# Rounding of the later batches as a chain over three engines, in a decoder layer on one Trainium2 core

## The reference

```
x = x + attention(layernorm(x))        # 32 heads, 8 key/value heads, causal, rotary
x = x + xattn(layernorm(x), context)   # the product below
x = x + moe(layernorm(x))              # 8 experts, capacity 256, plus a shared one, width 704

# xattn: both operands are rounded to float8 e4m3 in blocks, and scaled back
amax = max(abs(xb)) over 128 features of a token, at least 1e-4
q    = float8(xb * (448 / amax));  back = q * (amax / 448)
```

## Time and the profile before

| what | value |
|---|---|
| median of 3 runs | 1560.96 us (1559.98 to 1564.38) |
| profiled execution, its own time | 1559.33 us |
| its span, first to last instruction | 1557.5 us |
| mean granted TensorE clock | 0.982 |
| PE busy | 1445.0 us (93%) |
| DVE busy | 1188.3 us (76%) |
| POOL busy | 1024.0 us (66%) |
| ACT busy | 976.1 us (63%) |

### The profile page before, as it was taken

The page is one execution under the profiler, slowest core; times in us unless marked ns, Lnnn a source line. Parts: engine busy times, 40 slices in busy tenths (PEclk is TensorE's granted clock), DMA queues, the critical chain, the costliest instruction groups (busy, mean ns, idle before and its releaser), DMA issues.

```text
span 1557.5 us, 27023 instructions
## 1 busy us (share of the span) xinstructions
PE 1445.0 (93%) x8617; PEld 1263.8 (81%) x8617; DVE 1188.3 (76%) x2890; ACT 976.1 (63%) x2478; POOL 1024.0 (66%) x1027
## 2 busy tenths in 40 slices
PE   5899999999999999999999998977989897999997
PEld 4778888888878888778888887757888786999996
DVE  7678888887887887788888888787676755577775
ACT  4687777777677788878878787642121224556562
POOL 3787897887877888878988888434121213345455
PEclk9999999999999999999999999998999998999998
DMA  6435534333322433424434334222000004577777
GB/s 208 140 102 169 156 110 129 120 82 111 107 65 60 121 95 90 128 63 109 114 85 127 84 104 129 78 84 62 28 28 28 8 28 152 167 231 223 229 213 238
DMA packets 107964, 179.17 MB, mean 115 GB/s; under 512 B 17014, under 2 KB 38774, under 8 KB 107824
## 3 DMA queue, kind: packets, MB, share of 16 engines
q1 hardware_dynamic: 105072, 168.94, 37.0%
q0 software_dynamic: 2560, 8.25, 1.6%
q10 hardware_dynamic: 192, 0.26, 0.1%
HBM read 98.36 MB, written 33.03 MB: 84 GB/s over the span
## 4 chain that ended last, share of the span: by engine, by line
PE 62%; DVE 14%; ACT 12%; issue 6%; DMA 3%; POOL 2%; SPq 1%; DVEq 0%; POOLq 0%; ACTq 0%
PE bank L470 14%; PE bank L472 13%; PE bank L471 13%; PE bank L522 5%; ACT P L865 5%; PE bank L537 4%; PE bank L488 3%; PE bank L538 3%; PE bank L489 3%; DVE P L1191 2%; ACT PTh L877 2%; PE bank L462 2%; ACT Otmp L871 2%; DVE PTl L1232 1%; DVE Opair L1226 1%
## 5 line engine op out<-in xcount | busy, mean ns | idle before, releaser
L865 ACT ACTIVATE P<-P,mn 128x512 f32<-128x512 f32 (+3 forms) x512 | 284.5, 557 | 205.6 <-DVE mn L1191 201.8
L1636 POOL TENSOR_TENSOR P<-P,ri 128x128 f32<-128x128 f32 (+3 forms) x512 | 360.4, 735 | 30.8 <-DVE ri L1180 30.7
L1191 DVE CUSTOM_DVE_ANT_0 P<-bank,mask 128x512 f32<-128x512 f32 (+3 forms) x512 | 237.0, 481 | 84.1 <-PE bank L489 82.5
L1232 DVE TENSOR_TENSOR PTl<-bank,PTh 128x512 fp32r<-128x512 f32 (+1 forms) x384 | 229.9, 600 | 34.0 <-ACT PTh L877 31.3
L522 PE MATMUL bank<-ident,P 128*128 128x128 f32 x1280 | 201.4, 272 | 2.5 <-POOL P L1636 2.5
L877 ACT ACTIVATE PTh<-bank 128x512 fp32r<-128x512 f32 (+1 forms) x384 | 197.9, 517 | 3.5 <-PE bank L522 0.5
L488 PE MATMUL bank<-KT,QT 128*128 128x256 f32 (+2 forms) x512 | 187.6, 367 | 7.1 <-DVE mn L1191 7.1
L470 PE MATMUL bank<-XT,Wh 128*128 128x512 f32 x384 | 162.8, 424 | 9.2 <-DVE XT L1162 3.5
L537 PE MATMUL bank<-PTh,VS 128*128 128x256 f32 (+2 forms) x512 | 161.1, 326 | 6.8 <-DVE X L1241 2.4
L489 PE MATMUL bank<-KT,QT 128*128 128x256 f32 (+2 forms) x512 | 165.5, 323 | 0.0
L538 PE MATMUL bank<-PTl,VS 128*128 128x256 f32 (+2 forms) x512 | 154.6, 323 | 0.0
(11 more groups left out here) (224 smaller groups left out, 4160.5 us busy)
## 6 DMA issues: line engine op xcount, KB each, us to landing
RW<-in_wf SPq DMA_DIRECT2D x170, 256.0 KB, 3.0
QT<-qh SPq DMA_DIRECT2D x256, 64.0 KB, 2.0
QT<-ql SPq DMA_DIRECT2D x252, 64.0 KB, 2.0
Oraw<-in_wo SPq DMA_DIRECT2D x16, 512.0 KB, 4.7
KT<-KT SPq DMA_DIRECT2D x32, 256.0 KB, 3.0
Wraw<-in_wqkv SPq DMA_DIRECT2D x9, 768.0 KB, 5.0
xnx<-in_ctx SPq DMA_DIRECT2D x24, 256.0 KB, 3.6
saved<-Wh SPq DMA_DIRECT2D x7, 768.0 KB, 3.5
```

The costliest lines, as they stand in the source:

```text
L865: e.activation(pq, pq, ACT.Exp, bias=mn[:, z, qb:qb + 1], scale=-1.0, accum_out=rs[:, z, qb:qb + 1]).then_inc(a_exp, 1)
L1191: e.tensor_tensor_reduce(P[:, z, off[qb]:off[qb] + k], bank[n % 2][:, 0:k], mask[:, 512 - k:512], -0.125, BIG, ALU.add, ALU.min, mn[:, z, ...
L1232: e.tensor_tensor(pt_part(PTl, part), bank[2 + part][:, 0:128 * n].rearrange("p (m n) -> p m n", n=128), pt_part(PTh, part).bitcast(F32), ...
L1636: e.tensor_tensor(pq, pq, ri[:, z, qb:qb + 1].to_broadcast([128, n]), ALU.mult).then_inc(g_norm, 1)
```

## The change

For batches 1 to 3 the rounding is taken apart. ACT writes the normed tile (`look_later`, with a bias -mean/root that DVE computes once for a batch, `bias_of`); DVE takes its block maxima (`peaks`) one slot later; one set of scale steps serves all 4 tiles of a batch (`later_scales`); ACT multiplies by the scale, four activations to a tile (`scaled_later`); DVE's `rounded` keeps the two bit steps; POOL's three passes stay. The fourth tile of a batch is normed twice, for its maxima into the spare tile `T2[1]`, and again when its own buffer is free. A batch's first rounding is one slot earlier, its first transposes too; the fourth tile's come where they were. The scores and the choice of batch 0 move from slots -4 and -2 to -2 and 0, its places from 2 to 3.

```diff
-    plan(-4, "logits", 0)
-    plan(-2, "choose", 0)
-    plan(2, "place", 0)
+    plan(-2, "logits", 0)
+    plan(0, "choose", 0)
+    plan(3, "place", 0)
...
-            plan(s - 1 + i, "cross_round", b, i)
-            plan(s + 1 + i, "cross_turn", b, i)
-            plan(s + 2 + i, "cross_product", b, i)
-            plan(s + 3 + i, "stats3", b, i)
+
+            late = i // 3
+            plan(s - 8 + i, "look", b, i)
+            plan(s - 7 + i, "peaks", b, i)
+            plan(s - 3 + i + late, "scaled", b, i)
+            plan(s - 2 + i + late, "cross_round", b, i)
+            plan(s + i + late, "cross_turn", b, i)
+            plan(s + 1 + i + late, "cross_product", b, i)
+            plan(s + 2 + i + late, "stats3", b, i)
...
-        plan(s - 7, "norm2", b)
+        plan(s - 9, "norm2", b)
+        plan(s - 4, "scales", b)
...
+            def normed_by(dst, t):
+                e.activation(dst, X[:, t, :], ACT.Identity, bias=ssum[:, 0, t:t + 1],
+                             scale=rstd[:, t:t + 1]).then_inc(a_norm, 1)
+
+            def look_later(b, i):
+
+                need.wait_ge(v_small, 3 + 2 * b)
+                if i == 3:
+                    need.wait_ge(p_kv, NU)
+                    need.wait_ge(g_t2, TB * (b - 1))
+                    normed_by(T2[1], b * TB + i)
+                    return
+                need.wait_ge(p_turn, turn_at["cross_turn", b - 1, i or 3] + 1)
+                normed_by(T1[i], b * TB + i)
+
+            def scaled_later(b, i):
+                y = T1[i % 3]
+                if i == 3:
+                    need.wait_ge(p_turn, turn_at["cross_turn", b, 0] + 1)
+                    normed_by(y, b * TB + i)
+                need.wait_ge(v_small, 4 + 2 * b)
+                need.wait_ge(a_norm, normed_at(b, 4 if i == 3 else i))
+                for c in range(4):
+                    last = e.activation(y[:, tokens(c)], y[:, tokens(c)], ACT.Copy, scale=asc[:, i, 0, c:c + 1])
+                last.then_inc(a_scaled, 1)
...
-            def rounded(n, y, r):
+            def rounded(n, y):
                 q = T2[n % 2]
-                chain(e.tensor_tensor(four(y), four(y), r.unsqueeze(2).to_broadcast([128, 4, 128]), ALU.mult))
-                after()
+                need.wait_ge(a_scaled, len(jobs) + n + 1)
...
+            def bias_of(b):
+                ts = slice(b * TB, b * TB + TB)
+                after()
+                e.scalar_tensor_tensor(ssum[:, 0, ts], mv[:, ts, 0], -1.0, rstd[:, ts], ALU.mult,
+                                       ALU.mult).then_inc(v_small, 1)
+
+            def peaks(b, i):
+                need.wait_ge(a_norm, normed_at(b, i))
+                chain(e.tensor_reduce(aam[:, i, :], four(T2[1] if i == 3 else T1[i]), AX.X, ALU.max,
+                                      apply_absolute_value=True))
+
+            def later_scales(b):
+                need.wait_ge(a_kept, len(jobs))
+                need.wait_ge(g_q, TB * (b - 1))
+                after()
+                scales(aam[:, :, :], asc[:, :, 0, :], asc[:, :, 1, :], 1e-4).then_inc(v_small, 1)
```

More of the change, by code:

```diff
@@ L327, in turned_from @@
             if stage == "cross_turn":
-                return T1[(b * TB + i) % 3]
+                return T1[i % 3]
             return XN[:, i, :] if stage == "route_turn" else XE[:, b % 2, i, :]
@@ L332, in turn_bank, with normed_at @@
             return 6 if turns[n] in beside else other_at[turns[n]] % 2
+        def normed_at(b, i):
+            return TB + TB + 5 * (b - 1) + i + 1
         def wait_job_buffer(need, j):
@@ L943, in side_slot @@
                         logits(x[1])
+                    elif x[0] == "look":
+                        look_later(x[1], x[2])
+                    elif x[0] == "scaled":
+                        scaled_later(x[1], x[2])
             def split_piece(m, p):
@@ L1299, in large_steps_of @@
                 e.tensor_scalar(q, q, 2.0 ** -6, 1.5 * 2.0 ** 20, ALU.max, ALU.mult).then_inc(v_bq, 1)
[L1301 to L1307, removed]
-                after()
-                chain(normed(y, t))
-                after()
[L1311 to L1317, removed]
+            def bias_of(b):
+                ts = slice(b * TB, b * TB + TB)
+                after()
+                e.scalar_tensor_tensor(ssum[:, 0, ts], mv[:, ts, 0], -1.0, rstd[:, ts], ALU.mult,
[7 more added lines that the diff above has]
+                need.wait_ge(g_q, TB * (b - 1))
+                after()
+                scales(aam[:, :, :], asc[:, :, 0, :], asc[:, :, 1, :], 1e-4).then_inc(v_small, 1)
             def turn_lo(x):
@@ L1408, in side_slot @@
                         rstd_of(slice(b * TB, (b + 1) * TB))
+                        if stage == "norm2":
+                            bias_of(b)
+                    elif stage == "peaks":
+                        peaks(b, i)
+                    elif stage == "scales":
+                        later_scales(b)
                     elif stage == "cross_round":
-                        cross_round(b, i)
+                        rounded(round_at[x], T1[i % 3])
                     elif stage == "norm3":
@@ L1724, in side_slot @@
                     if stage == "cross_round":
-                        rounded(round_at[x], T1[(b * TB + i) % 3], asc[:, i, 1, :])
+                        rounded(round_at[x], T1[i % 3], asc[:, i, 1, :])
                     elif stage == "place":
```

## The result

| | before | after |
|---|---|---|
| median | 1560.47 us (1558.22 to 1564.38, 4 runs) | 1551.67 us (1549.08 to 1552.82, 4 runs) |
| span of the profiled execution | 1557.5 us | 1550.2 us |
| its granted clock, mean | 0.982 | 0.986 |
| busy: PE, DVE | 1445.0, 1188.3 us | 1444.4, 1167.0 us |
| busy: POOL, ACT | 1024.0, 976.1 us | 1020.8, 999.0 us |

The ratio is 0.9939, with a 95% interval of 0.992 to 0.9959. That is 8.8 us less in the medians, against a forecast of 1551.4 and 9.6 us less. DVE is relieved of 21 us, ACT takes on 23, PE's work is the same.

What follows compares the result with a forecast made beforehand. PE's waits, chiefly for POOL's third pass, with constants, DVE's additions and lost clock, were taken to bound the three batch steps. Gains of 6.3 + 2.3 + 1.0 = 9.6 us gave 1551.4; forecast 1546 to 1556, full range 1542 to 1561.

Steps and rivals of the forecast that it cites:

- Its value is how much sooner POOL starts.: DVE work removed ahead of POOL's passes, within 4.96 us in batch 2, is worth only POOL's earlier start.
- Batch 1, 6.3 us: Batch 1's step: third product ends at 1091.8 against 1098.09, so 6.3 us gained, trusted to 3 us either way.
- with no wait for constants: Batch 1: with scores two slots later PE runs up steps and scores without waiting for constants, saving 2.70 us.
- Batch 2, 2.3 us: Batch 2's step: turn waits 1.5 and 2.55, product wait 0.9, none before the places; 2.3 us gained.
- Down 6.93 + 1.6: Batch 2's 30 down matmuls: 6.93 us plus 1.6 for the low clock kept behind closely spaced waits.
- Batch 3, 1.0 us: Batch 3's step: the same 24.6 us as batch 2 in place of 25.56, so 1.0 us gained.
- kept its pace: Evidence for the POOL-rate rival: behind batch 3's waits at the places the stretch ended 1.33 us sooner than batch 2's.
- ScalarE: ACT's added 28 us is covered by its waits for PE; rival that it delays the silu: 1567, chance 0.08.
- Table loads: Norms on ACT bring no new table loads; otherwise two of 1.28 us each, up to 38 us.
- Nothing but POOL's rate: Rival: no held bit step or low-part wait, PE keeps its clock; 2.9 us more a batch, 1543, chance 0.15.
- The wait only moves: Rival: turns 1.85 us apart on PE want POOL chains of 3.9, so waits return; 1562, chance 0.19.

Runs made afterwards that it cites:

- e2: The changed kernel with scores, choice and places of batch 0 back in slots -4, -2 and 2; 1557.26 us, ratio to before 0.9963.
- e10: The kernel before, fused rounding kept on DVE, with the rounding of tiles 0 to 2 one slot earlier; 1568.98 us, ratio to before 1.0034.
- e1: The kernel before with only scores, choice and places of batch 0 moved to slots -2, 0 and 3; 1557.94 us, ratio to before 0.9966.
- e5: The changed kernel with tiles 0 to 2 of batches 1 to 3 normed again on ACT before scaling; 1551.98 us, ratio to before 0.9934.
- e3: The changed kernel with turns, products and statistics of tiles 0 to 2 one slot later, as before the change; 1538.96 us, ratio to before 0.9857.
- e8: The changed kernel with turns, products and statistics of tiles 0 to 2, and bit steps of tiles 2 and 3, one slot later; 1534.35 us.
- e12: e8 with the inverse roots (norm2) of batch 1 also one slot later; 1536.41 us, ratio to before 0.9828.
- e11: e12 with batch 1's tile 0 turn, product and statistics and tile 3 scaling and bit steps one more slot later; 1540.56 us.
- e6: The changed kernel with the inverse roots (norm2) of batch 1 one slot later; 1550.51 us, ratio to before 0.9922.
- e14: The changed kernel with only the bit steps of tiles 2 and 3 one slot later; 1548.98 us, ratio to before 0.9921.

## Why the prediction was right

The time (1551.4, measured 1551.67) and the sign were right, and in batches 2 and 3 so was the mechanism. That the 9.6 us came so near the measured 8.8 is in part luck: batch 1 was forecast 2.9 us too high, batches 2 and 3 together 2.2 too low.

- **"Its value is how much sooner POOL starts."** Right, and well sized: POOL's first pass was forecast 16.75 us into batch 2 and came at 16.73. e2 shows the worth of it in batches 2 and 3, and e10 that the same slot with the old rounding gives nothing.
- **Batch 1, 6.3 us.** Mis-sized: 3.4. By the step's own account the third product should have ended 47.8 us after the first up step; it ended at 50.47 (1099.65 less 1049.18). The difference lies ahead of the first turn, which came 25.57 us in, not 23.1. The step "with no wait for constants" failed: they came 9.2 us in (5.1 before), 4.1 later where I had said 2.3. The rows for this, SP's issues in the changed kernel:

```profile
1053.25 0.33 SPq L2075 DMA_DIRECT2D Graw<-in_wg  x1
...
1054.10 0.43 SPq L2077 DMA_DIRECT2D tri<-in_tri  x1
```

and what ACT did with them:

```profile
1058.40 0.23 ACT L1121 ACTIVATE Gh<-Graw 128x32 fp32r<-128x32 f32 x1 [3.25 <-DMA tri<-in_tri]
```

The issue came 2.0 us later than before (4.07 after the first up step against 1048.85 less 1046.80), about what I had said. But from the issue of the last load to ACT it took 4.3 us (1054.10 to 1058.40) where it had taken 2.2 (1049.70 to 1051.90), and I had no term for that; its cause is not shown. In the eight kernels that issue it at the same 4.9 us, that time was anything from 2.4 (e2) to 4.3, so how much of it belongs to the change is open. I had the constants at 7.4 us and the turn 15.7 behind them; they were at 9.22 and the turn 16.35 behind (table above), so 1.8 of the 2.5 us are the constants' lateness and 0.7 the chain behind them. PE's own waits ahead of the turn, 1.48 for the constants and 1.26 for DVE's product with the silu (L1498, behind tile 3's maxima and the four scale steps, 1063.60 to 1065.4), I did not have either, but they do not add to this, as PE then stood another 5.51 for POOL (forecast 5.8). Behind the turn, the half up step took 2.71 (1.45), the second turn did not wait (1.75), the low part's wait was 1.77 (0.5) and the down stage took 6.82 (8.5), so that stretch came to 24.9 us against 24.7.
- **What the scores' move is worth.** I had it inside the 6.3 with no price of its own. e1 gives it 4.3 us, and batch 1 of e2 is 4.2 longer than the change's: as much as batch 1's whole gain.
- **Batch 2, 2.3 us.** Under-sized: 3.5. The first turn waited 1.23 (1.5) and the second 2.30 (2.55), and they came 20.8 and 25.1 us in, as forecast (20.8 and 25.2). The low part held nothing (0.9), the wait behind the places was 1.16 (1.6). "Down 6.93 + 1.6" put the slow clock in the wrong place but near the right size: the product lost 1.5 (4.36 less 2.84) and the down stage ran at 1.00.
- **Batch 3, 1.0 us.** Under-sized, 2.0, by the same terms. That batch 2 gained 1.5 more than batch 3 comes from before: its product behind the places took 4.25 us in batch 2 and 2.83 in batch 3, and in e1 the other way round. The prediction's "kept its pace" is this, so it was no sign for the rival that leaned on it.
- **ScalarE.** Right that the 28 us (27.0 measured: 15.3 for the scaling, 11.7 for the norms) have cover in batches 2 and 3: e5 put nine norms more on it, 7.2 us, and the turns there waited no longer.
- **Table loads.** Right: no norm brought one. Over the whole span silu's line has two loads, as before, and the norms' line none. ACT loaded its table once before the first silu, and later norms ran under it:

```profile
1059.55 1.28 ACT L1011 ACT_TABLE_LOAD   x1
...
1120.18 0.82 ACT L906 ACTIVATE work<-X,ssum,rstd 128x512 f32<-128x512 f32 x1 [2.47 <-DVE ssum L1343]
```

The Trainium skill (ScalarE: Activation LUTs, Table sets: the hidden batching unit) says that the cheap functions are in every set; the trace agrees, as 15 norms ran with no load at their line.

- **The rivals.** "Nothing but POOL's rate" did not come: the bit steps were held, and the waits were there. "The wait only moves" did not decide the time, but e3 shows that it was at work: of what the change frees, the earlier turns spend more (12.7 us) than it keeps (8.8). My steps priced the new waits rightly and never asked what the old slots would have given; the profile of before had the answer, since two turns 1.85 us apart on PE want chains that take 3.9 on POOL.

What stays open is how to shorten batch 1's chain. e3, e8 and e12 leave 3.7 to 3.8 us of wait for POOL at the first turn, e11 shows DVE late behind it, and no run here moved ACT's and DVE's weight pieces or batch 0's choice of experts away from that stretch. Why the constants' loads took longer than before is open too.

## What to carry to other kernels

When a chain of engines is made to start sooner, leave its consumers where they are first, and move them only if the trace then shows them idle for want of order, not of data; consumers that come closer together than the slowest stage's time per tile only turn the gain into waits. A wait's releaser is the last of perhaps several: take it away in an experiment and look who stands 0.4 us behind before you price its removal. Compare when the awaited event comes, not how long the wait is: e5's first turn waited 0.7 us longer than the change's and came no later. And a move that looks like housekeeping (here the scores' two slots) should be run alone, as it may carry a whole term of the sum.

## What the runs showed of the hardware

A DVE instruction beside POOL was held, not slowed in proportion: the bit steps of 128x512 with one SBUF input took 0.42 us with POOL idle, and 1.15 to 1.37 beside its passes of 1.1 to 1.4. The one issued at 1147.55 ended at 1148.73, POOL's pass at 1148.45; the one issued at 1148.76 ended at 1149.91, POOL's pass at 1149.62. I had expected this of instructions with two SBUF inputs first. In e10 the norm took 0.54 us free and 1.15 beside POOL, while the reduce of 128x512 issued at 1157.52, within POOL's pass of 1157.28 to 1158.38, took its usual 0.69: so not every instruction is held. The Trainium skill (SBUF — State Buffer, SBUF: two separate sides) says that the shared pair of ports is locked for a whole instruction and the loser waits for it; the trace agrees, with those ends.

The clock fell for a product behind short waits, and did not in all cases with the same ones. Batches 2 and 3 of the change, e2, e5, e6 and e14 give ten stretches with turn waits of 1.21 to 1.33 and 2.25 to 2.32 us. In seven the product behind them took 4.17 to 4.43 us, in three (batch 2 of e5 and e14, batch 3 of e6) 2.85. No run here says what decides it, so a term of 1.5 us a batch can't be forecast from the waits alone, and a difference of 1.5 us in one profiled batch step proves nothing about an edit.
